# The first expert layer of a four-layer model: all experts for all tokens, or 63 gathered tiles of chosen pairs

## The reference

```python
def _L0_ffn_ref(x, gate_w, gate_b, w1, b1, w2, b2, w3, b3, ws1, bs1, ws2, bs2, ws3, bs3):
    E, D, H, TOP_K = 16, 256, 176, 6                  # shared part: hidden 2 * 176
    probs = jax.nn.softmax(xf @ gate_w.T, axis=-1)
    _, idx = jax.lax.top_k(probs + gate_b, TOP_K)
    weights = jnp.take_along_axis(probs, idx, axis=1)
    cw = jnp.einsum('tk,tke->te', weights, jax.nn.one_hot(idx, E))
    def expert_step(y, params):
        h = jax.nn.silu(xf @ W1.T + B1) * (xf @ W3.T + B3)
        return (y + c[:, None] * (h @ W2.T + B2), None)
    y, _ = jax.lax.scan(expert_step, zeros, (w1, b1, w2, b2, w3, b3, cw.T))
    z = jax.nn.silu(xf @ ws1.T + bs1) * (xf @ ws3.T + bs3) @ ws2.T + bs2
    return y + z
```

## Time and profile before

| what | value |
|---|---|
| median of 3 runs | 1167.91 us |
| the profiled execution, and its span | 1165.65 us, 1163.9 us |
| TensorE busy | 85% of the span |
| first expert layer | from 285 to 580 us of the span |
| folding of layer 1's weights | from 580 to 636 us |
| last expert layer | from 953 us to the end |

### The profile page before, as it was taken

How to read it: one execution, slowest core, us unless ns; L and a number is a source line. 1 busy time by engine, 2 the same in 40 slices (tenths; PEclk the granted TensorE clock), 3 DMA queues, 4 the chain that set the end, 5 groups by cost and what they waited for, 6 DMA issues and landing times. The chain is left out here.

```text
span 1163.9 us, 14272 instructions
## 1 busy us (share of the span) xinstructions
PE 990.9 (85%) x5133; PEld 795.6 (68%) x5133; DVE 672.4 (58%) x1105; ACT 354.6 (30%) x541; POOL 353.8 (30%) x244
## 2 busy tenths in 40 slices
PE   2999999868779999999788995967726869999996
PEld 2677787658568899998667894755615656566664
DVE  4466666545385556655634888968677853222221
ACT  2234443222522333333223442334313432222121
POOL 2577776400122222222100220153235310512222
PEclk9899999969889999999878996969956988999999
DMA  3111120001111111110081001000010019622220
GB/s 113 72 39 39 38 77 0 1 1 35 45 46 46 46 45 45 45 45 18 2 256 61 29 1 33 1 1 1 0 41 1 1 53 399 245 63 42 40 34 10
DMA packets 21473, 61.40 MB, mean 53 GB/s; under 512 B 4401, under 2 KB 12866, under 8 KB 19074
## 3 DMA queue, kind: packets, MB, share of 16 engines
q1 hardware_dynamic: 17346, 56.55, 14.3%
q0 software_dynamic: 4080, 4.22, 2.2%
HBM read 55.50 MB, written 9.21 MB: 56 GB/s over the span
## 5 line engine op out<-in xcount | busy, mean ns | idle before, releaser
L914 DVE SCALAR_TENSOR_TENSOR ffn_HF<-ffn_U,ffn_BIAS,ffn_HG 128x512 f32<-128x512 f32 x54 | 40.4, 750 | 82.5 <-ACT ffn_HG L797 82.4
L87 PE MATMUL ffn_DN<-ffn_WDS_hi,ffn_HS_hi 128*128 128x256 f32 x288 | 83.6, 290 | 3.9 <-DVE ffn_HS_lo L922 3.3
L797 ACT ACTIVATE ffn_HG<-ffn_G,ffn_UB 128x512 f32<-128x512 f32 x54 | 37.1, 690 | 160.5 <-PE ffn_U L89 160.1
L2160 PE MATMUL ffn_GU<-ffn_W,ffn_XTB 128*128 x184 | 85.0, 605 | 0.1
L88 PE MATMUL ffn_DN<-ffn_WDS_lo,ffn_HS_hi 128*128 128x256 f32 x288 | 83.3, 289 | 0.0
L89 PE MATMUL ffn_DN<-ffn_WDS_hi,ffn_HS_lo 128*128 128x256 f32 x288 | 83.2, 289 | 0.0
L767 POOL TENSOR_TENSOR ffn_WDS_lo<-ffn_WD,ffn_WDS_hi 128x1024 fp32r<-128x1024 f32 x9 | 22.1, 2461 | 200.2 <-ACT ffn_WDS_hi L787 200.2
L929 DVE SCALAR_TENSOR_TENSOR X<-ffn_DN,ffn_CG,X 128x256 f32<-128x256 f32 x144 | 67.3, 480 | 20.6 <-PE ffn_DN L89 12.5
L1980 POOL DMA_INDIRECT out_x<-ffn_YB,ffn_XB x23 | 35.9, 1560 | 113.7 <-DVE ffn_YB L2109 111.7
L464 DVE TENSOR_TENSOR attn_RP<-attn_QB,attn_COS 96x1024 f32<-96x1024 f32 x32 | 39.0, 1218 | 51.3 <-PE attn_QB L89 51.2
L2098 DVE COPY ffn_XTB<-ffn_XP 128x256 f32<-128x256 f32 x23 | 9.8, 425 | 88.0 <-PE ffn_XP L2169 88.0
(11 more groups left out here) (432 smaller groups left out, 2759.6 us busy)
## 6 DMA issues: line engine op xcount, KB each, us to landing
ffn_W<-in_f_w SPq DMA_DIRECT2D x9, 1536.0 KB, 27.9
attn_W<-in_L_pairs SPq DMA_DIRECT2D x8, 1088.0 KB, 5.0
ffn_WU<-in_f_up SPq DMA_DIRECT2D x9, 768.0 KB, 4.2
ffn_WD<-in_f_down SPq DMA_DIRECT2D x9, 512.0 KB, 3.5
expert_rows<-in_rows_empty SPq DMA_DIRECT2D x1, 2967.0 KB, 14.4
ffn_XB<-expert_rows SPq DMA_DIRECT2D x23, 129.0 KB, 2.1
ffn_STAGE<-in_f_w SPq DMA_DIRECT2D x1, 2048.0 KB, 8.2
ffn_STAGE<-in_L_pairs SPq DMA_DIRECT2D x2, 768.0 KB, 7.3
```

Source lines behind the costliest of these rows:

```text
L87: pe.matmul(out, a[0], b[0], start=first, stop=False)
L797: act.activation(HG[:, k % 2, :], G[:, k % 2, :], ACT.Silu, bias=bias).then_inc(silu_done, 1)
L914: dve.scalar_tensor_tensor(out=HF[:, k % 2, :], in0=U[:, k % 2, :], scalar=BIAS[:, bass.ds(e * (2 * NC) + 2 * m + 1, 1)], in1=HG[:, k % 2, ...
L2160: last = pe.matmul(GU[:, m, :], x, weights(e, k * 2 * HID3 + m * HID3, HID3), start=k == 0, stop=k == KD - 1)
```

## The change

The first expert layer is computed by a new function, `routed_many`:

- SyncE writes the normalised tokens to DRAM (`rows0`, one more row of zeros), and behind them in the same row the 16 weights of each token.
- The shared part is computed for 8 token tiles. Between these, VectorE picks the six experts (`choose`), counts places (`place`), and marks places as one-hot matrices (`mark`, 8 times 128 x 2048). TensorE multiplies the one-hots (`enlist`, 8 times 16 products with 16 columns): the result is each expert's list of tokens. `owners`, `lists` and `index` turn it into 63 columns of 128 row numbers (`IDX`) and each tile's expert (`EI`). 63 is 6144 / 128 + 15, so that it is enough for any distribution; all 63 tiles are always computed, unused places with the row of zeros.
- For each of the 63 tiles GpSimd gathers 128 rows of 272 numbers from DRAM with an indirect DMA into one of NB = 4 buffers `XB`. TensorE, VectorE and ScalarE compute the expert with float32 products (biases by a row of ones and by VectorE), ScalarE weighs the result (`weigh`), and GpSimd scatters it with addition into `sum_a` (even tiles) or `sum_b` (odd tiles).
- SyncE puts X with the shared part into `sum_a` (`base_out`). In `latent_chain`, SyncE reads both sums back, VectorE adds and measures them, and the normalisation moves from the first to the second round there.
- The 3 MB fill of `expert_rows` (now `rows3`), a fill of `sum_b` and the row of zeros are issued in attention 0. XT lives in inner contexts; a clearing of semaphores moves.

The core of the diff:

```diff
-        experts("f0", 4, 9, 3, 16, 6, True)
+        clear_semaphores()
+        routed_many(4)
...
+                        def gather(i):
+                            if i >= NB:
+                                pool.wait_ge(y_ready, i - NB + 1)
+                                pool.wait_ge(x_turned, i - NB + 1)
+                            pool.indirect_dma_start(XB[:, i % NB, :], None, DR["rows0"][:, :], bass.IndirectOffsetOnAxis(ap=IDX[:, i:i + 1], axis=0)).then_inc(rows_in[i % NB], 16)
+                        def scatter(i):
+                            pool.wait_ge(y_ready, i + 1)
+                            if i >= 2:
+                                pool.wait_ge(sums_done[i % 2], 16 * (i // 2))
+                            pool.indirect_dma_start(DR["sum_b" if i % 2 else "sum_a"][:, :], bass.IndirectOffsetOnAxis(ap=IDX[:, i:i + 1], axis=0),
+                                                    YB[:, i % NY, :], None, bounds_check=B * S - 1, oob_is_err=False, compute_op=ALU.add).then_inc(sums_done[i % 2], 16)
+                        pool.wait_ge(rows_out, 16)
+                        pool.wait_ge(weights_out, 16)
+                        pool.wait_ge(idx_ready, 1)
+                        AHEAD = NB - 1
+                        for i in range(AHEAD):
+                            gather(i)
+                        pool.wait_ge(base_out, 16)
+                        for i in range(NT):
+                            if i + AHEAD < NT:
+                                gather(i + AHEAD)
+                            scatter(i)
...
+                        def weigh(n, e):
+                            i = n - T
+                            act.wait_ge(down_done, n + 1)
+                            if i >= NY:
+                                act.wait_ge(sums_done[i % 2], 16 * ((i - NY) // 2 + 1))
+                            act.activation(YB[:, i % NY, :], DN[:, n % 2, 0:D], ACT.Copy, scale=XB[:, i % NB, bass.ds(D + e, 1)]).then_inc(y_ready, 1)
...
+                        def mark(t):
+                            if t >= NM:
+                                dve.wait_ge(listed, t - NM + 1)
+                            dve.tensor_tensor(OHA[:, t % NM, :, :], PLACES[:, :].unsqueeze(1).broadcast_to((P, E, P)),
+                                              POS[:, 4, t, :].unsqueeze(2).broadcast_to((P, E, P)), ALU.is_equal).then_inc(places_marked, 1)
...
+                        def turn_x(n):
+                            i = n - T
+                            pe.wait_ge(rows_in[i % NB], 16 * (i // NB + 1))
+                            if i > 0:
+                                pe.wait_ge(x_out, i)
...
+                        for n in range(ITEMS + 2):
+                            if n == T:
+                                pe.wait_ge(w_in, 16 * E)
+                                pe.wait_ge(owners_out, 1)
+                            if n < ITEMS:
+                                owner[n] = None if n < T else pe.value_load(EI[0:1, n - T:n - T + 1], min_val=0, max_val=E - 1)
+                                up(n, owner[n])
+                            if n == 1:
+                                count()
+                            for t in LIST_AT.get(n, ()):
+                                enlist(t)
+                            if n == T - 1:
+                                turn_h(n - 1)
+                                down(n - 2, None)
+                                index()
+                            if n + 1 >= T and n + 1 < ITEMS:
+                                turn_x(n + 1)
+                            if 1 <= n <= ITEMS and n != T - 1:
+                                turn_h(n - 1)
+                            if n >= 2 and n != T - 1:
+                                down(n - 2, owner[n - 2])
...
-                NORM_AFTER = 1
+                NORM_AFTER = 2
...
+                            if g == 1:
+                                for i, (dst, src) in enumerate(((X, "sum_a"), (XN, "sum_b"))):
+                                    sp.wait_ge(sums_done[i], 16 * ((TILES0 + 1 - i) // 2))
+                                    sp.dma_start(dst[:, :, :], DR[src].rearrange("(t p) d -> p t d", p=P)).then_inc(taken[i], 16)
```

More of the change, by code:

```diff
@@ L89, in mm3, with program @@
     return pe.matmul(out, a[1], b[0], start=False, stop=last)
-def program(nc, A, out, rows_dram):
+def program(nc, A, out, DR):
     with ExitStack() as top:
@@ L1143, in _ @@
                                 dve.tensor_tensor(g_part(g, h, 1), g_bank(h), g_part(g, h, 0).bitcast(F32), ALU.subtract).then_inc(g_lo, 1)
+                            if g == 0:
+                                for i in range(2):
+                                    dve.wait_ge(taken[i], 16)
+                                for t in range(T):
+                                    dve.tensor_tensor(X[:, t, :], X[:, t, :], XN[:, t, :], ALU.add).then_inc(whole, 1)
+                                    dve.wait_ge(whole, t + 1)
+                                    measure(dve, stats, t).then_inc(measured, 1)
+                            if g == NORM_AFTER - 1:
+                                nrm["vector"](dve)
                             if g == NORM_AFTER:
@@ L2307, in fold_pairs, with expert_weights, up, down @@
     return w
-def expert_pairs(a):
-    n, hid = 18, 176
-    up = np.zeros((n // 2, P, 3, KD, 2, P), np.float32)
-    down = np.zeros((n // 2, P, 4, D), np.float32)
-    bias = np.zeros((P, n // 2, 3, 2), np.float32)
-    for e in range(n):
-        if e < 16:
-            g, u, gb, ub, d = a["w1"][e], a["w3"][e], a["b1"][e], a["b3"][e], a["w2"][e]
-        else:
-            s = slice(hid * (e - 16), hid * (e - 15))
-            g, u, gb, ub, d = a["ws1"][s], a["ws3"][s], a["bs1"][s], a["bs3"][s], a["ws2"][:, s]
-        p, j = divmod(e, 2)
-        for chunk, tile, to, rows in ((2 * j, 3 * j, 0, slice(0, P)), (1, 1 + j, 64 * j, slice(P, hid))):
-            k = rows.stop - rows.start
-            for m, w in ((0, g), (1, u)):
-                up[p, :, chunk, :, m, to:to + k] = w[rows].T.reshape(KD, P, k).transpose(1, 0, 2)
-            down[p, to:to + k, tile] = d[:, rows].T
-            bias[to:to + k, p, chunk, 0], bias[to:to + k, p, chunk, 1] = gb[rows], ub[rows]
-    return up.reshape(n // 2, P, -1), down.reshape(n // 2, P, -1), bias.reshape(P, -1)
+def expert_weights(a):
+    def up(g, u):
+        return np.concatenate([g.T.reshape(KD, P, -1), u.T.reshape(KD, P, -1)], 2).transpose(1, 0, 2).reshape(P, -1)
+    def down(w, b, chunks):
+        rows = np.zeros((chunks * P, D), np.float32)
+        rows[:w.shape[1]], rows[w.shape[1]] = w.T, b
+        return rows.reshape(chunks, P, D).transpose(1, 0, 2).reshape(P, -1)
+    each = np.stack([np.concatenate([up(a["w1"][e], a["w3"][e]), down(a["w2"][e], a["b2"][e], 2)], 1) for e in range(E0)])
+    shared = np.concatenate([up(a["ws1"], a["ws3"]), down(a["ws2"], a["bs2"], 3)], 1)
+    return each, shared
 def layout(i):
@@ L2375 @@
     out = nc.dram_tensor("out_x", (B * S, D), F32, kind="ExternalOutput").ap()
-    rows_dram = nc.dram_tensor("expert_rows", (TILES3 * P, ROW3), F32, kind="Internal").ap()
-    program(nc, aps, out, rows_dram)
+    shapes = {"rows3": (TILES3 * P, ROW3), "rows0": (B * S + 1, ROW0), "sum_a": (B * S, D), "sum_b": (B * S, D)}
+    scratch = {n: nc.dram_tensor("scratch_" + n, shape, F32, kind="Internal").ap() for n, shape in shapes.items()}
+    program(nc, aps, out, scratch)
     r = run_bass_kernel_spmd(nc, [arrays], core_ids=[0])
```

752 lines of the change are left out of this document (395 added, 357 removed).

## The result

| | before | after |
|---|---|---|
| median of 4 runs each, us | 1168.84 | 1561.87 |
| lowest to highest, us | 1162.71 to 1170.90 | 1558.58 to 1563.89 |
| ratio of the medians, 95% interval | | 1.337, 1.331 to 1.343 |
| span of the profiled execution, us | 1163.9 | 1556.8 |

The forecast was 1508, the range 1405 to 1590. The change costs 393 us.

What follows compares the result with a forecast made beforehand. The old layer was held bound by TensorE's products, the new one by a closed circle of waits. New stretch 75 + 22 + 525 + 9 = 631 us against 295: 1165.65 + 336 + 6 = 1508 us, range 1405 to 1590.

Steps and rivals of the forecast that it cites:

- The mechanism: In the 63-tile loop, each result waits for a whole gather issued only after the result before it; forecast 60%.
- the turn: Tile loop, from one tile's weighed result to the next: 8.9 us at the low clock, 59 times, 525 us.
- the circle: Tile loop: result, scatter, gather three tiles ahead, TensorE's transposes and `down`, weighing, next result; closed, at 8.9 us.
- Rival 3, the open circle: Tile loop: gathers run ahead, GpSimd's own work sets the pace, 3.12 us a tile, 1176 us in all; chance 5%.
- the folding: Folding of layer 1's weights: VectorE's additions and measuring add 8.8 us between first and second round, 6 of them standing.
- Rival 1, the high clock: Tile loop: TensorE keeps its high clock, 7.6 us a tile, 1431 us in all; chance 18%.
- the two reasons given for the low clock: TensorE in the tile loop: busy about 5 of 8.9 us, and idle 3.8 us at a stretch; clock 0.50.
- Rival 2, the dear gather: Tile loop: gather takes 1.56 us on GpSimd and lands later, 10.9 us a tile, 1626 us; chance 14%.
- Ahead of the loop: First expert layer before its tile loop: 75 us to the first gather, then 22 us to the first result.
- the marks' price: VectorE ahead of the tile loop: eight `mark` at 2.28 us, 18.3 us; the other end, 3.38 each, adds 9.
- Behind it: After the tile loop: the last three results need no gather, four scatters are left, 9 us.
- 3 of the 8.8 covered: Second round of the folding: 3 of VectorE's 8.8 added us fall in time the moved normalisation or a wait took before.

## Why the prediction was right, and what its steps were worth

- **The mechanism** (a result waits for a whole gather that is issued behind the result before it) was right. It is shown, not argued: each list's order shortens the turn by itself (6.48 and 7.03 a tile), look-ahead spreads the circle over more tiles until it no longer sets the pace (4.31, 3.22), and buffers alone do nothing (9.55).
- **Rival 3, the open circle**, did not come, for the reason that was given. Its price was right in size: 3.12 a tile and 1176 forecast, 3.11 and 1170.87 measured with look-ahead 7. That the totals meet so closely is partly luck: the layer took 284.8 us there (299 forecast) and the folding 69.2, 14 more than before (6 forecast).
- **Rival 1, the high clock**: the clock fell to 0.51. Its price was right in size: 77 forecast, 89 measured, 82 of them in the 59 turns. One of the two reasons given for the low clock doesn't hold: TensorE's busy share does not tell the clock, and with the gather ahead of the scatter it stayed at 0.52 at a share of 81% (the rows are at the end). The other reason, an idle stretch longer than the one of 3 us after which it had fallen, agrees with the change (3.9 us), but with the gather ahead of the scatter the clock stayed low although TensorE waited only 1.4 us a turn in the mean (70 of 360 us, 51 turns). So the level was right, with some luck, since the reasons don't carry it.
- **Rival 2, the dear gather**: it lands in 2.9 us (3.0 forecast). By the Trainium skill's formula (DMA: Bandwidth & Descriptors, section on the anatomy of a software DMA) it was estimated at 2.3; the measured number decides, and a plain load plus GpSimd's own 0.96 was the nearer guide.
- **Ahead of the loop**: 67.7 us to the first gather (75 forecast). The other end of the marks' price, 3.38 each, did not come. From there to y(0) 24.0 (22).
- **The term that was too small is the turn**: 8.9 forecast, 9.55 measured, 38 us over 59 turns. Of the 0.65, 0.23 are the gathers of one and the same row (9.55 against 9.32). The other 0.42 are within 0.05 TensorE's part, 3.26 against a forecast of 2.8, while the rest of the turn (1.27 + 1.59 + 0.31 and a gather of 2.9) comes within 0.05 of its forecast. The transposes take 610.55 - 609.64 = 0.91, forecast 0.88; `down` was priced as products without a gap, 1.73 at the low clock, and takes 2.21. In the rows of `down` the weight load of its second half stands behind 0.65 "issue", 0.33 at the high clock. What makes the gap was not tested. It isn't the expert's address alone, which is read from a register: the last layer reads it so too, and in the kernel before the eight loads of its `down` stand without a gap:

```profile
1132.96 1.60 PEld L2187 LDWEIGHTS ffn_DN<-ffn_W,ffn_HT 128*128 128x128 f32 x8
```

There all loads have 128 rows, here the second half has 49.

- **Behind it**: 11.0 to the end of the last scatter on GpSimd (9 forecast), and then 3.3 us in which no engine runs before the next block begins, which the sum did not have. The last scatter, which lands 2.7 us after its start, covers 1.1 of them:

```profile
948.91 1.56 POOL L1980 DMA_INDIRECT scratch_sum_a<-ffn_YB,ffn_IDX  x1 [0.30 <-issue]
953.81 1.36 SPq L737 DMA_DIRECT2D layer_STAGE<-in_L_pairs  x3
953.81 0.74 POOL L745 MEMSET chain_AF<- 128x768 f32 x1 [3.34 <-POOLq L1943]
```

- **The folding**: +6 forecast, +19.4 measured, the step that failed most by its own measure. VectorE in order of time there:

```profile
976.87 0.43 DVE L787 TENSOR_TENSOR X<-X,XN 128x256 f32<-128x256 f32 x1 [0.84 <-DMA XN<-scratch_sum_b]
...
984.80 0.41 DVE L773 COPY chain_AF<-chain_PB 128x256 f32<-128x256 f32 x1
...
996.94 1.38 DVE L240 TENSOR_SCALAR XN<-X,MOM,RSTD 128x256 f32<-128x256 f32 x4
```

The eight additions with their measures last 984.80 - 976.87 = 7.9 us, 0.9 less than forecast, but none of it is covered: the second round's copy, which TensorE waits for, stands behind it. "3 of the 8.8 covered" was wrong, and the moved normalisation (3 us from 996.73) has lost the hole that it filled. Part of the rest is TensorE's clock. It was 0.68 over the folding of the change, and 0.77 in the run with rows of zeros of its own, whose folding has the same lists and took 68.6 us instead of 74.5. So 5.9 of the 19.4 go with the clock, up to 8.5 are the piece on the path, and some 5 are left, of which the normalisation can be 3.

Against its own base the sum was 393 - 342 = 51 us short. The turn's 38 and the folding's 13 are all of it: the preparation's 7 too many are made up by 2 to y(0), 2 in the tail and the 3.3.

## What to carry to other kernels

Write down for each pair of engine lists how many tiles one runs ahead of the other; a look-ahead on a loading engine opens a circle only if it is longer than that of the engine that consumes, here 4 or more against 3, and buffers without it change nothing. A queue that carries loads and write-backs ties each load to a result. And where products are cut to save work, ask what clock the rest runs at, and which engine is full next: here 63 tiles on GpSimd at 3.2 us are 202 us, and with what must be done ahead of them the layer is nearly as long as the dense one was.

## What the runs showed of the hardware

- Fixed prices of GpSimd's indirect DMAs in this shape: a gather of 128 rows of 272 numbers is 0.99 us on GpSimd and lands 2.8 to 2.9 after its start (at look-ahead 3); a scatter with addition is 1.59 and lands in 3.8 in the median; 0.30 lies between two.
- Scatters whose places all lie out of bounds, those of the empty tiles, cost GpSimd the same 1.56 to 1.59 and land in 2.8 (the change, 862 to 935 us; three of these four are of empty tiles):

```profile
scratch_sum_a<-ffn_YB,ffn_IDX POOLq DMA_INDIRECT x4, 2.8
```

- 128 places that read one row land in 3.7 to 4.1 instead of 2.9.
- A scatter with addition starts 0.80 to 0.84 after the result it waits for (20 cases in the change), a gather 0.27 to 0.28 (26 cases with the gather ahead of the scatter).
- The busy share doesn't tell the clock. TensorE was busy 347 of 575 us in the change at 0.51, 267 of 340 with the other order on its list at 0.64, and, in the columns of the earlier trace rows, 81% with the gather ahead of the scatter at 0.52, and 80% with look-ahead 4 at 0.91:

```profile
400.00:760.00 360.00, 290.45 (x617) 146.73 (x616) 61.59 (x154) 61.96 (x155) 134.54 (x104) 0.52 0.23 37
```

```profile
400.00:620.00 220.00, 176.55 (x624) 97.32 (x624) 62.19 (x155) 60.53 (x155) 133.70 (x104) 0.91 0.35 58
```

The low clock itself makes the products long, and so the share high.
